# State space stage: the spread rows of B and C alternate between two PSUM banks, and B is spread a step ahead

## What is computed

```python
D_STATE = 16
EXPAND = 2
D_INNER = EXPAND * D_MODEL
...
x_dbl = xs @ W_x
d_raw = x_dbl[..., :1]
Bp = x_dbl[..., 1:1 + D_STATE]
Cp = x_dbl[..., 1 + D_STATE:]
delta = jax.nn.softplus(d_raw * w_dt + b_dt)

def step(h, inp):
    dt, b, c, xt = inp
    At = jnp.exp(dt[..., None] * A)
    h = At * h + (dt * xt)[..., None] * b[:, None, :]
    y = jnp.einsum('bdn,bn->bd', h, c)
    return (h, y)
```

## Time and profile before

| | |
|---|---|
| runs of the kernel before | 3414.5 us median of 3 (3413.73 to 3419.38) |
| the profiled execution | 3416.19 us, its span 3414.4 us |
| the first and the last u of the state space stage | 1751.5 and 2439.6 us from the span's start |
| busy over the whole span | PE 74%, DVE 65%, ACT 44%, POOL 33% |
| mean granted TensorE clock | 0.822 |

### The profile page before, as it was taken

One profiled execution on the slowest core, in us unless ns is written; L12 is line 12 of the kernel. 1 busy time (PEld: TensorE's weight loads), 2 busy tenths in 40 slices (PEclk: granted clock), 3 DMA queues, 4 the chain that ended last, 5 costly groups with the idle time before them and its releaser, 6 DMA issues. The chain is left out here.

```text
span 3414.4 us, 49243 instructions
## 1 busy us (share of the span) xinstructions
PE 2524.0 (74%) x17446; PEld 1269.1 (37%) x17454; DVE 2234.6 (65%) x4562; ACT 1497.3 (44%) x2911; POOL 1138.9 (33%) x1172
## 2 busy tenths in 40 slices
PE   3999987874898876775557777677624846899986
PEld 1333334442444445554522222222214842233334
DVE  4888868784667644342368887888742237888854
ACT  1777761110555542222344444444311214777751
POOL 3222104432221202232435555555573433222001
PEclk9999997775899986556877877777856976999989
DMA  5111100000211201005800000000014942212100
GB/s 161 32 39 28 31 1 0 1 0 19 42 31 38 45 25 39 14 19 169 255 9 1 0 0 0 0 0 1 0 35 158 292 145 43 48 30 41 20 4 22
DMA packets 129156, 157.01 MB, mean 46 GB/s; under 512 B 18000, under 2 KB 110288, under 8 KB 128304
## 3 DMA queue, kind: packets, MB, share of 16 engines
q1 hardware_dynamic: 119248, 139.91, 15.7%
q0 software_dynamic: 6592, 13.56, 1.1%
q10 hardware_dynamic: 3072, 0.40, 0.1%
HBM read 95.56 MB, written 25.59 MB: 35 GB/s over the span
## 5 line engine op out<-in xcount | busy, mean ns | idle before, releaser
L422 DVE TENSOR_REDUCE a_mx<-banks 128x1 f32<-128x512 f32 (+3 forms) x1536 | 882.6, 618 | 253.3 <-PE banks L762 123.1
L633 ACT ACTIVATE a_prob<-banks 128x512 f32<-128x512 f32 (+3 forms) x1536 | 773.9, 545 | 382.4 <-PE banks L785 156.9
L785 PE MATMUL banks<-a_Qs,a_Ks 64*128 64x512 bf16 (+3 forms) x1536 | 512.6, 368 | 48.1 <-ACT a_prob L633 40.9
L762 PE MATMUL banks<-a_Ks,a_Qs 63*128 63x512 bf16 (+3 forms) x1536 | 503.1, 375 | 45.7 <-DVE a_mx L422 32.7
L813 PE MATMUL banks<-a_prob,a_vaug 128*32 128x256 f32 (+2 forms) x5632 | 446.3, 390 | 0.7 <-ACT a_prob L633 0.5
L2073 PE MATMUL banks<-m_hc,kc 128*128 128x512 f32 x512 | 340.5, 765 | 118.5 <-POOL m_hc L1949 99.5
L1949 POOL TENSOR_TENSOR m_hc<-m_h,m_cs 128x512 f32<-128x512 f32 x256 | 327.9, 1297 | 287.0 <-DVE m_h L1813 274.7
L1996 ACT ACTIVATE banks<-m_dt,acoef 128x512 f32<-128x512 f32 x256 | 175.8, 691 | 297.2 <-DVE m_h L1813 296.9
L1813 DVE TENSOR_TENSOR_SCAN m_h<-banks,m_u 128x512 f32<-128x512 f32 x256 | 301.6, 1209 | 0.0
L762 PEld LDWEIGHTS banks<-a_Ks,a_Qs 63*128 63x128 bf16 x1536 | 126.7, 95 | 406.0 <-DVE a_mx L422 220.7
L1798 DVE TENSOR_TENSOR m_u<-m_dtx,banks 128x1024 f32<-128x1024 f32 x128 | 155.3, 1213 | 104.6 <-PE banks L2054 102.0
(11 more groups left out here) (405 smaller groups left out, 4730.3 us busy)
## 6 DMA issues: line engine op xcount, KB each, us to landing
c_wbuf<-in_w2e SPq DMA_DIRECT2D x71, 512.0 KB, 4.2
b_wbuf<-in_w1e SPq DMA_DIRECT2D x39, 578.0 KB, 4.4
a_Ks<-a_parts SPq DMA_DIRECT2D x288, 64.0 KB
a_Qs<-a_parts SPq DMA_DIRECT2D x288, 64.0 KB
rows_in<-in_unused SPq DMA_DIRECT2D x1, 4579.5 KB, 16.7
c_yb<-rows_in SPq DMA_DIRECT2D x71, 64.5 KB, 4.8
a_mixed_in<-rows_back SPq DMA_DIRECT2D x16, 256.0 KB, 3.9
a_Qs<-a_negm ACTq DMA_DIRECT2D x192, 2.0 KB
```

What stands on the lines that cost most here:

```text
L422: dve.tensor_reduce(mx[:, g % 2, col:col + 1], M[:, k % 3, 0:keys[j]], AX.X, ALU.max).then_inc(S("max_read"), 1)
L633: act.activation(prob[:, n % 8, first_query[kt]:T], Sc[:, n % 2, first_query[kt]:T], ACT.Exp, scale=scale).then_inc(S("exped"), 1)
L762: i = pe.matmul(M[:, k % 3, 0:keys[j]], Qs[lo:lo + LAST, b % 4, pair, j * P:(j + 1) * P], Ks[lo:lo + LAST, b % 4, pair, 0:keys[j]], start= ...
L785: i = pe.matmul(Sc[:, n % 2, q0:T], Ks[lo:lo + HALF, b % 4, pair, kt * P:(kt + 1) * P], Qs[lo:lo + HALF, b % 4, pair, q0:T], start=True, s ...
```

## The change

One pair of banks, `R`, takes the place of `Bs` and `Cs`. B(k) goes to bank k mod 2 and C(k) to bank (k+1) mod 2. B(k+1) therefore goes to the bank where C(k) was, and its spread now waits for cs(k); C(k) goes to the bank where B(k-1) was and waits for u(k-1). On PE C(k) is due at at(k) - 5.6 and B(k+1) at at(k) - 4.2; on ACT cs(k) at at(k) - 5.5. The number of instructions is the same on every engine. The orders of DVE, POOL and the queues are as before.

```diff
--- before.py
+++ after.py
@@ -1770,7 +1770,7 @@
                 G, mid, rest = room("G", [96, 2, T], BF16), room("mid", [96, T], BF16), room("rest", [96, T])
                 stats, mom, small = room("stats", [P, NT, 6]), room("mom", [P, 2, NT, 2]), room("small", [P, 2, 4, NT])
                 flat = banks.rearrange("p a b t -> p (a b) t")
-                Y, Bs, Cs, A, X = flat[:, 0:2, :], flat[:, 2, :], flat[:, 3, :], flat[:, 4:6, :], flat[:, 6:8, :]
+                Y, R, A, X = flat[:, 0:2, :], flat[:, 2:4, :], flat[:, 4:6, :], flat[:, 6:8, :]
 
                 used = {}
 
@@ -1795,7 +1795,7 @@
                             dve.wait_ge(S("dtx_ready"), b + 1)
                         if k >= 3:
                             dve.wait_ge(S("scanned"), NCH * (k - 2))
-                        dve.tensor_tensor(u[:, k % 3], dtx[:, b % 2], Bs.unsqueeze(1).broadcast_to([P, NCH, T]),
+                        dve.tensor_tensor(u[:, k % 3], dtx[:, b % 2], R[:, k % 2, :].unsqueeze(1).broadcast_to([P, NCH, T]),
                                           ALU.mult).then_inc(S("u_ready"), 1)
 
                     for k in range(DS * B + 1):
@@ -1979,11 +1979,11 @@
                 def scalar_scan(act):
                     for k in range(DS * B):
                         b = k // DS
-                        yield at(k) - 2.8
+                        yield at(k) - 5.5
                         act.wait_ge(S("c_spread"), k + 1)
                         if k >= 4:
                             act.wait_ge(S("weighed"), NCH * (k - 3))
-                        act.activation(cs[:, k % 4, :], Cs, ACT.Copy).then_inc(S("c_taken"), 1)
+                        act.activation(cs[:, k % 4, :], R[:, (k + 1) % 2, :], ACT.Copy).then_inc(S("c_taken"), 1)
                         for c in range(NCH):
                             yield at(k) + 1.2 * (c + 1) - 3.4
                             n = NCH * k + c
@@ -2045,22 +2045,28 @@
                     act.activation(mid[64:96, :], rest[64:96, :], ACT.Copy).then_inc(S("mid_part"), 1)
 
                 def tensor_scan(pe):
-                    def spread(k):
+                    def spread_b(k):
                         b, n = divmod(k, DS)
                         if n == 0:
                             pe.wait_ge(S("parted"), b + 1)
                         if k:
+                            pe.wait_ge(S("c_taken"), k)
+                        pe.matmul(R[:, k % 2, :], kb("sel32", 96)[:, n:n + 1].broadcast_to([96, P]), G[:, b % 2, :],
+                                  start=True, stop=True).then_inc(S("b_spread"), 1)
+
+                    for k in range(DS * B):
+                        b, n = divmod(k, DS)
+                        if k == 0:
+                            yield at(k) - 8.2
+                            spread_b(0)
+                        yield at(k) - 5.6
+                        if k:
                             pe.wait_ge(S("u_ready"), k)
-                        pe.matmul(Bs, kb("sel32", 96)[:, n:n + 1].broadcast_to([96, P]), G[:, b % 2, :], start=True,
-                                  stop=True).then_inc(S("b_spread"), 1)
-                        if k:
-                            pe.wait_ge(S("c_taken"), k)
-                        pe.matmul(Cs, kb("sel32", 96)[:, DS + n:DS + n + 1].broadcast_to([96, P]), G[:, b % 2, :],
-                                  start=True, stop=True).then_inc(S("c_spread"), 1)
-
-                    for k in range(DS * B):
-                        yield at(k) - 3.4
-                        spread(k)
+                        pe.matmul(R[:, (k + 1) % 2, :], kb("sel32", 96)[:, DS + n:DS + n + 1].broadcast_to([96, P]),
+                                  G[:, b % 2, :], start=True, stop=True).then_inc(S("c_spread"), 1)
+                        if k < DS * B - 1:
+                            yield at(k) - 4.2
+                            spread_b(k + 1)
 
                 def tensor_sums(pe):
                     for k in range(DS * B):
```

## The result

The change runs in 3384.59 us (median of 4 runs, 3380.27 to 3387.2) beside 3415.35 us for the kernel before on the same chip (4 runs, 3413.73 to 3419.38). The ratio is 0.9907, with a 95% interval of 0.989 to 0.9924: faster by about 31 us. The forecast was 3387, in a range of 3370 to 3406. The profiled execution, the fastest of the four, took 3380.27 us, its span is 3378.5 us.

A forecast was written before the change was run, and what follows sets the result against it. Limits differed by stretch: PE behind the output projection, ACT in silu, DVE in softplus, a chain at batch ends. Terms 13.4 + 2 + 10 + 1.9 = 27.3 us off 3416.2, less 1.7: 3387; own range 3377 to 3398, whole 3370 to 3406.

The forecast's parts named there:

- The part that buys nothing: Projection stretch and silu: u waits of 0.40 and 6.28 us bring no direct gain; silu's becomes waits for decays and G.
- Term 1: Seven silus: ACT reaches the table load earlier, six by 1.87 us and the first by 2.2; 13.4 us, bounds 0 to 17.
- Term 2: Gate matmuls in silu: less PE idle time keeps the clock up more often; 2 us, bounds 0 to 5.7.
- Term 3: Batch ends: four of seven lose DVE's wait for the new batch's first B; 10 us, yf's chain gains nothing, bound 6.
- It holds no wait for B: Chain from yf to residual sum: no wait for B, so earlier u only lengthens the wait for line 2120; no gain.
- Term 4: Last batch, with no next projection beside it: its 1.87 us wait for B is gained whole; 1.9 us.
- More than that: Silu, clock, yf chain, batch ends and tail all at their bounds: about 41 us gained, 3374 us; chance 0.18.
- The wait only changes its name: Silu really waits for the last projection matmul, so only batch ends and tail gain, 12 us: 3402 us; chance 0.15.
- Slower: PE's B ahead of L2117 waits for ACT's copy and delays G at half clock: +10 us, 3424; chance 0.05.
- It does nothing: The u waits are for something other than B's spread, so time stays 3414.5 us; chance 0.05.
- The signs: Expected: L2054 waits under 15 us, 3 to 5 us of ACT waits a batch, table-load distances about 4 us shorter.

The follow-up runs named there:

- the run that moved the ends: The change's order with the old banks, plus DVE's normalization pieces for batches 4 to 7 moved from softplus into silu's wait: 3365.21 us, ratio 0.9856.
- the fourth experiment: The change plus four small unused 128x128 copies on ACT ahead of each silu group, against the kernel before: 3379.92 us, ratio 0.9908.

## Why the prediction was right, and where not

The time, 3384.59, lies in the forecast's own range, 2.4 us from it. By its terms it was less exact: several errors cancelled, and that the number came so close is luck. The stage fell by 31.7 us where the terms gave 27.3: 13.8 for the first term as mended below, 4.3, 17.6 and 2.6 for the others, 0.7 more between decays and remainder, less 7.4 that the forecast had at nothing.

**The part that buys nothing** held. The 6.28 us wait for B became 4.20 for the decay and 2.49 for G, and the remainder stands 5.60 us behind the decays, as said. The two waits together, 6.7 us, are more than the 3 to 5 us forecast. They were not all fixed, which I had not looked at: filling G's gave 11.7 us.

**Term 1, an earlier silu, 13.4 us.** Measured are 10.4: the first and second row of the table, 1.3 and 9.1 (1.5 for each of six, not 1.87). The mechanism was right, and PE's limit came in: the copy ahead of the table load waited 0.59 us for its spread. A piece of the sum was missing besides. I booked the copy's 0.58 us as a cost ahead of the table load but not as a gain behind silu, where it no longer stands ahead of the decays. The best case there fell from 6.46 to 5.97: 7 x 0.49 = 3.4 us. With it the term is 13.8.

**Term 2, the clock, 2 us.** Measured 7.7 - 3.4 = 4.3, within the bounds of 0 to 5.7. All seven gate stretches are at full clock. The Trainium skill's page "TensorE: Matmul & The Clock Gate", section "The HAM clock gate (the "warmup" mystery)", has the throttled clock as the default and activity as what releases it; by that, less idle time takes the upper bound. The traces agree in direction: none slow of 63 places without idle time, 2 of 7 with 1.95 us of it. I had leaned to the lower bound because the same 2.20 us had come before both durations. That showed only that a gap of that size is uncertain; it said nothing of no gap, and there was none, not the 0.4 us that I had reckoned. My upper bound took 1.43 us for all four, where they were 0.65, 1.44, 1.64 and 0.58. The 3.42 us that I called the longest was not: batch 5 had 3.62, and 8.09 us from table load to decays.

**Term 3, the batch end, 10 us.** Measured 17.6. In the four later batches remainder to yf is 4.0 us shorter: 2.4 to 2.6 by the first u's B, as forecast, 10.2 in four, and most of the rest by yf's chain, whose short form came (3.05 us from line 2006, where I had reckoned 3.4 to 4.3 and taken the long end). This chain got 0.7 to 1.4 us shorter, 7.6 together, at six ends and not at seven: the seventh, batch 6's, has no transpose beside it (the order shown for such places ahead of the prediction holds for six). The step that failed was the choice of the long end. The seventh stretch became 1.2 us longer, since yf waits 1.47 us there where it had waited for nothing: the next step's B, which waits for ACT's copy, stands ahead of the batch's last sum, as the rows of the result show.

**"It holds no wait for B".** That step was wrong, and it is the one with the other sign. The prediction let the chain from yf to the residual sum stand, as DVE has no wait for B in it. But PE has: B of the next step now stands in PE's list ahead of the output projection and waits for ACT's copy. With the sum behind it, that is 4.8 of the 7.4 us; the other part is the projection itself, 3.5 us longer at a lower clock. I had found this very pattern, a spread that waits ahead of a matmul on the chain, before L2117, and made it the slower rival, and not looked for it at the output projection. With a B that waits for u instead of the copy, this stretch is 3.1 us shorter, 1.3 of it by an earlier start and 1.8 by a shorter projection. With the projection ahead of both, in the experiment that moved it, it starts 0.05 us behind the gating as before the change, and the stretch is still 6.1 us longer, as the projection is 7.0 us longer at the lower clock. That the wait is what lowers the clock is not shown: the small unused copies ahead of silu left 4.3 us of the late start, and the projection took 19.0 us all the same, less than the 19.5 of before.

**Term 4, 1.9 us.** Measured 2.6.

**The rivals.** "More than that" came near in its parts on the clock (4.3 of 5.7) and true on yf (7.6 beside 6), and not in the whole, which also had silu at its bound and left out the +7.4. "The wait only changes its name" fell with 10.4 us in term 1. "Slower" did not decide: L2117 ended 4.84 us after the decays' start, against its limit of 5.0. "It does nothing" fell, but the experiments split the change: its banks do nothing alone, ACT's earlier copy alone costs, and the order of all three, without the banks, gives the whole gain.

**The signs.** u's waits for L2054, the table load against the last L2099 and the remainder behind the decays came as said. From one silu's table load to the next the later batches shrank by 5.5 to 7.0 us, not about 4: term 1, the clock and yf's chain each gave more there than reckoned. Yf waits 2.3 us, not some 3.

## What to carry to other kernels

Where engines take their work in order, ask of every early instruction what it waits for and what stands behind it in the same list: a producer moved ahead helps only if its own releaser is ahead too, and each further place that it passes has to be looked at, on the engine that issues it and not only on the one that waited. A buffer that is shared by turns ties two streams together (B to ACT's copy here) and can cost more than it frees; try the order alone before the buffers. When a large wait splits into smaller ones for other things, those are places for work that is due soon after.

## What the runs showed of the hardware that was not expected

**VectorE beside GpSimd.** Four `tensor_scalar` of 128x128 took 4.09 us in the kernel before beside products on POOL, and 1.11 us with POOL idle in the run that moved the ends. One by one the four took 2357, 1299, 336 and 335 ns: the first ended 0.08 us after POOL's product of 2.34 us (2095.61), the second 0.08 us after the next, line 1949's (2096.83), and beside the last two POOL did nothing. The kernel before:

```profile
2093.27 2.34 POOL L1974 TENSOR_TENSOR m_dtx<-m_dt,m_xs 128x1024 f32<-128x1024 f32 x1
2093.33 4.09 DVE L1852 TENSOR_SCALAR m_back_in<-m_back_in,m_mom,m_small 128x128 f32<-128x128 f32 x4
```

The run that moved the ends:

```profile
2041.23 1.04 POOL L1872 TENSOR_TENSOR m_small<-m_small,mhalf 128x4 f32<-128x4 f32 x1
2042.30 1.11 DVE L1852 TENSOR_SCALAR m_back_in<-m_back_in,m_mom,m_small 128x128 f32<-128x128 f32 x4 [2.92 <-POOL m_small L1872]
```

Over the 16 of them in the stage, min/mean/max in ns:

The kernel before:

```profile
L1852 DVE TENSOR_SCALAR m_back_in<-m_back_in,m_mom,m_small x16: 333/817/2359, 1997.6 to 2286.9; 128x128 f32<-128x128 f32 x16
```

The run that moved them:

```profile
L1852 DVE TENSOR_SCALAR m_back_in<-m_back_in,m_mom,m_small x16: 340/342/347, 1956.6 to 2214.6; 128x128 f32<-128x128 f32 x16
```

That is 16 x 0.475 = 7.6 us of DVE's time in a stretch that DVE bounds, and may be part of what moving them gained; no run separates it. The Trainium skill's page "GPSIMD Engine Reference", section "1. Specifications", names GpSimd's SBUF interfaces as shared with VectorE, with contention for some of VectorE's instructions; the trace agrees, and gives the price.

**PE's clock at equal idle time.** The same 2.20 us of idle time was followed by matmuls of 1.99 and of 3.42 us, and 2.71 us by 1.99 in three of seven and up to 3.68 in the others; 1.95 us by the lower clock in two of seven; 0.67 us or none in none of 70.

**Small copies on ACT.** Four copies of 128x128 took 0.89 us and moved the table load by 0.77; four of 128x512 took 2.18, 0.55 each. This made the fourth experiment miss.
